# Three runs of score tiles in the projection stage: from behind the first keys to behind the last values of their block

## What is computed

```
q = (layernorm(x) @ Wq + bq)   # 512 queries, 16 heads of 32
k = (y @ Wk + bk)              # 8192 keys
v = (y @ Wv + bv)              # 8192 values
scores = q k^T * scale
attn = softmax(scores, axis=-1)
out = attn @ v ; h = relu(out @ W1 + b1) ; result = h @ W2 + b2
```

## Time and profile before

| | us |
|---|---|
| median of three runs | 1423.57 |
| the profiled execution | 1425.03 |
| its span | 1423.1 |
| PE busy | 1346.2 (95%) |
| DVE busy | 1143.0 (80%) |
| ACT busy | 815.2 (57%) |
| POOL busy | 787.1 (55%) |
| mean granted clock of TensorE | 0.982 |

### The profile page before, as it was taken

One profiled execution on the slowest core, in us unless ns is written; L12 is line 12 of the kernel. 1 busy time (PEld: TensorE's weight loads), 2 busy tenths in 40 slices (PEclk: granted clock), 3 DMA queues, 4 the chain that ended last, 5 costly groups with the idle time before them and its releaser, 6 DMA issues. The chain is left out here.

```text
span 1423.1 us, 39397 instructions
## 1 busy us (share of the span) xinstructions
PE 1346.2 (95%) x16766; PEld 720.1 (51%) x16766; DVE 1143.0 (80%) x1834; ACT 815.2 (57%) x1531; POOL 787.1 (55%) x307
## 2 busy tenths in 40 slices
PE   7989988998999999999999999999999999887898
PEld 4444444443655555555555555555555444556444
DVE  7668877888888888888888888888886664676797
ACT  4445434543777777766776777777777632573212
POOL 3322221222999988998898899989986002000111
PEclk9999999999999999999999999999999999999999
DMA  7567876776352122112212221222120030950000
GB/s 260 169 165 222 231 191 179 214 219 177 93 183 67 38 67 65 52 52 67 63 35 62 65 67 37 68 65 64 40 71 2 18 127 7 202 126 1 1 8 23
DMA packets 127790, 137.44 MB, mean 97 GB/s; under 512 B 44992, under 2 KB 108992, under 8 KB 125696
## 3 DMA queue, kind: packets, MB, share of 16 engines
q1 hardware_dynamic: 127616, 134.93, 33.3%
HBM read 75.66 MB, written 44.17 MB: 84 GB/s over the span
## 5 line engine op out<-in xcount | busy, mean ns | idle before, releaser
L1285 DVE TENSOR_REDUCE early<-attend_banks 128x1 f32<-128x512 f32 x952 | 612.4, 685 | 82.7 <-PE attend_banks L1031 77.5
L1249 ACT ACTIVATE attend_prob<-attend_banks 128x512 f32<-128x512 f32 x1024 | 536.0, 599 | 202.2 <-PE attend_banks L1068 200.0
L1429 POOL TENSOR_TENSOR early<-early,attend_prob 128x1024 f32<-128x1024 f32 x210 | 614.5, 2926 | 37.7 <-ACT attend_prob L1249 9.6
L1068 PE MATMUL attend_banks<-early,k_first 97*32 97x512 f16 x2560 | 261.8, 384 | 3.1 <-ACT attend_prob L1249 3.1
L1031 PE MATMUL attend_banks<-k_first,early 96*32 96x512 f16 x2272 | 236.4, 384 | 1.1 <-PEq L282 1.1
L1031 PE MATMUL attend_banks<-attend_k_rest,early 96*32 96x512 f16 x1536 | 157.6, 380 | 0.0
L1068 PE MATMUL attend_banks<-early,attend_k_rest 97*32 97x512 f16 x1536 | 154.4, 381 | 2.8 <-ACT attend_prob L1249 2.8
L1092 PE MATMUL attend_banks<-attend_prob,ones 128*32 128x128 f32 x3048 | 135.1, 273 | 3.6 <-DVE attend_recip L1297 3.6
L500 POOL TENSOR_TENSOR project_w_whole<-project_grid,project_qscale 128x704 f32<-128x704 f32 x24 | 33.3, 1386 | 183.6 <-DVE project_grid L630 183.6
L1081 PE MATMUL attend_banks<-attend_prob,wkv_area 128*32 128x512 f32 x1024 | 134.8, 592 | 0.0
L1081 PE MATMUL attend_banks<-attend_prob,attend_vh_odd 128*32 128x512 f32 x1024 | 133.7, 592 | 0.0
(11 more groups left out here) (191 smaller groups left out, 1870.4 us busy)
## 6 DMA issues: line engine op xcount, KB each, us to landing
v_scratch<-project_v SPq DMA_DIRECT2D x16, 1024.0 KB, 8.6
early<-in_ctx_dram SPq DMA_DIRECT2D x16, 768.0 KB, 6.1
k_first<-k_scratch SPq DMA_DIRECT2D x36, 256.0 KB, 3.4
k_scratch<-project_k_hi SPq DMA_DIRECT2D x64, 128.0 KB, 3.0
k_scratch<-project_k_lo SPq DMA_DIRECT2D x64, 128.0 KB, 3.1
attend_vh_odd<-v_scratch SPq DMA_DIRECT2D x8, 1024.0 KB, 4.8
wkv_area<-v_scratch SPq DMA_DIRECT2D x7, 1024.0 KB, 4.9
attend_k_rest<-k_scratch SPq DMA_DIRECT2D x24, 256.0 KB, 3.4
```

The lines of the kernel that those rows point to most:

```text
L1068: last = nc.tensor.matmul(s_ps[c * HD:(c + 1) * HD, s_bank[n], :], key_rows[:, c * HD:(c + 1) * HD], q_stack[0:KROWS + 1, h, :], start=Tru ...
L1249: nc.scalar.activation(prob[:, q % PSLOTS, t, :], s_ps[:, s_bank[BT * q + t]], ACT.Exp, scale=SCALE).then_inc(p_ready, 1)
L1285: nc.vector.tensor_reduce(part_max[:, s, j, part:part + 1], pre_ps[:, bank], AX.X, ALU.max).then_inc(pre_read, 1)
L1429: nc.gpsimd.tensor_tensor(sums, sums, prob[:, q % PSLOTS, 0:n], ALU.add).then_inc(pool_summed, 1)
```

## The change

The position KEYS_0 is given up and a position VALUES_3, behind the last value tile, is added. The tiles of head 1's parts 0 and 1 move from KEYS_0 to VALUES_3 of the same blocks, 8 and 10. In block 3 head 0's part 1 goes to VALUES_1 and part 2 to VALUES_3; before they were at KEYS_0 and VALUES_1. VectorE reads the tiles of VALUES_3 in the next block, two behind the low half of key group 0 and its quantization step, two behind group 1's. The tiles of VALUES_3 wait for the low half of the next block's y, as those of VALUES_1 do.

```
-            KEYS_0, KEYS_2, VALUES_1, VALUES_2 = range(4)
-            part_at = {(2, VALUES_1): (0, 0), (3, KEYS_0): (0, 1), (3, VALUES_1): (0, 2), (8, KEYS_0): (1, 0), (10, KEYS_0): (1, 1)}
+            KEYS_2, VALUES_1, VALUES_2, VALUES_3 = range(4)
+            part_at = {(2, VALUES_1): (0, 0), (3, VALUES_1): (0, 1), (3, VALUES_3): (0, 2), (8, VALUES_3): (1, 0),
+                       (10, VALUES_3): (1, 1)}
...
                             key_low(i, u, g)
                             if g < 3:
                                 quantize(1)
-                            if g >= 1:
-                                maxima(b, KEYS_0, range(2 * g - 2, min(2 * g, TT)))
+                            maxima(b - 1, VALUES_3, range(2 * g, min(2 * g + 2, TT)))
                         maxima(b, KEYS_2)
...
-                        pe.wait_ge(ylo_ready, min(b + (2 if place == VALUES_1 else 1), NB))
+                        pe.wait_ge(ylo_ready, min(b + (1 if place == KEYS_2 else 2), NB))
...
                         last.then_inc(k_ready, 1)
-                        if g in (0, 2):
-                            maxima(2 * i + u, (KEYS_0, None, KEYS_2)[g])
+                        if g == 2:
+                            maxima(2 * i + u, KEYS_2)
...
                         last.then_inc(v_ready, 1)
-                        if t in (1, 2):
-                            maxima(2 * i + u, VALUES_1 if t == 1 else VALUES_2)
+                        if t >= 1:
+                            maxima(2 * i + u, (VALUES_1, VALUES_2, VALUES_3)[t - 1])
```

## The result

| | before | after |
|---|---|---|
| median, first comparison (5 runs each), us | 1423.63 | 1413.22 |
| lowest to highest | 1420.21 to 1425.62 | 1412.94 to 1414.64 |
| span of the profiled execution | 1423.1 | 1411.2 |
| mean granted clock | 0.982 | 0.989 |

The account below looks back on a forecast made before the run. TensorE, busy 95% of the span, was taken as the bound, through its idle and slow time. Gains of 3.3, 4.4 and 4.8 us sum to 12.5: 1425.03 becomes 1412.5, less 1.46 for the median gives 1411.1 us, range 1407.0 to 1415.5.

Parts of the forecast that it names:

- The cause: At the transposes of blocks 3, 8 and 10, VectorE's queued score-tile reads are late and hold TensorE, 12.9 us in sum.
- (a) The moved tiles' wait: Moved tiles on TensorE wait for the same block's VALUES_1 reads: 0.90 us in blocks 8 and 10, 0.14 in block 3.
- (b) Block 4: At block 4's transposes, a new wait of 2.1 us replaces the old 3.45; gain 3.3 us over blocks 3 to 5.
- (c) Blocks 9 and 11: At these blocks' transposes, a new wait of 0.75 us; the two pairs gain 4.4 and 4.8 us.
- The clock term: Granted clock does not fall at the new waits; a fall in block 4, up to 2.7 us, had chance 0.13.
- The wait only moves: Rival: reads in blocks 4, 9, 11 stay late, TensorE waits 3.45 to 4.7 us, clock falls; 1423 us, chance 0.07.
- Slower: Rival: in blocks 4 to 11 moved reads delay key stores, so head 0 tiles wait; 1429 us, chance 0.05.
- No new wait: Rival: VectorE's reads come in time, each place costs only its 0.865 us; gain 17.1, time 1406.5 us, chance 0.09.

Follow-up runs that it names:

- block 3 alone: Against the kernel before, only block 3's run of tiles was moved, blocks 8 and 10 keeping theirs behind the first keys; 1421.88 us, ratio 0.9982.
- the runs in blocks 3, 7 and 9: Against the changed kernel, the runs of blocks 8 and 10 put behind the last values of blocks 7 and 9; 1414.32 us, ratio 0.9927 to the kernel before.
- early reads in odd blocks: Against the kernel before, tiles behind the first keys read a key group earlier, runs of blocks 8 and 10 moved to 9 and 11; 1405.8 us, ratio 0.9871.

## Why the prediction was right

**The cause** was right, and is now shown from both sides: early reads at the old place gave 12.7 us, the new place with late reads gave none. The lag of 0.80 us from the start of the third read to the transposes held: 0.79 in block 4 (117.83 to 118.62) and in block 9 (211.16 to 211.95) of the change, 0.79 in block 4 of the new place without early reads.

**(a) The moved tiles' wait** was forecast as 0.90 of delay; it is 0.76 of idle time, which with the 0.16 by which a matmul's record runs over is 0.92. In block 3 the forecast was 0.14; the block takes 18.84 us where 18.64 is its time without a wait (early reads at the old place), so 0.20.

**(b) Block 4.** The replay held step by step. With T = 107.71 (89.91 + 17.80), VectorE after:

```profile
115.84 0.96 DVE L602 TENSOR_TENSOR project_k_lo<-early,project_k_hi 128x512 f16<-128x512 f32 x1
116.72 0.51 DVE L622 TENSOR_SCALAR project_qr<-project_qn 128x704 uint32<-128x704 uint32 x1
117.26 0.53 DVE L624 TENSOR_SCALAR project_qr<-project_qr 128x704 f32<-128x704 f32 x1
117.83 0.69 DVE L646 TENSOR_REDUCE early<-project_yT_ps 128x1 f32<-128x512 f32 x1
```

The low half starts at T + 8.1, the rounder at T + 9.0, the third read at T + 10.1, the transposes (118.62) at T + 10.9, each as forecast. The low half lasts 0.96 instead of 0.68: it starts while GpSimd multiplies (114.86 to 116.24) and ends 0.56 us behind it, as the 1.60 of the earlier trace rows ended 0.55 behind GpSimd's end. The "SBUF — State Buffer" page of the Trainium skill, section "SBUF: two separate sides", says that a GpSimd operation and a VectorE operation with two SBUF inputs exclude each other for a whole instruction; these two rows agree. Gain 3.2 us against 3.3 forecast.

**(c) Blocks 9 and 11.** A delay of 0.75 was forecast; the transposes start at 211.95 where 203.48 + 7.77 = 211.25 would be without a wait, 0.70 (0.53 of idle time in the row, for which the prediction named 0.6 to 0.8). Gains 4.4 and 4.8, as forecast.

**The clock term** was right in part by luck. The forecast took no fall at a wait of 2.1 us, by the nearest row, and gave 0.13 to a fall. Six waits of 1.92 or 1.93 us stand in the profiles of this study (one each in the change's two profiles and with block 3 alone, three with the runs in blocks 3, 7 and 9): the clock fell behind two of them. Of the two waits of 2.09 and 2.10, it fell behind one. So the falls came more often than 0.13 says. The price is 1.7 us, where the prediction bounded it by 2.7. The changed kernel is at the edge here, and an execution of it may well be 1.7 us longer than its profiled one. Of its five runs in the first comparison three had spans of 1411.2 to 1411.4 us at a mean clock of 0.988 or 0.989 and two had 1412.6 and 1412.7 at 0.986; whether block 4 makes this difference was not traced.

**The rivals.** "The wait only moves" is what the place without the reads does: 11.5 us of waits in blocks 4, 9 and 11. It failed because the change also moved the reads up. "Slower" by late stores: the waits that a landing of `k_scratch` ends are two, both in block 15, before as after, 0.58 and 1.19 before, 0.36 and 1.36 after. The stores gained no weight. "No new wait" did not hold for the change, but is what early reads in odd blocks reach: blocks 3 to 5 take 55.19 us there and both pairs 37.39, 17.1 us less than before in sum, as that case has it.

**The size.** 12.5 forecast, and 12.5 and 12.4 in the projection of the two profiles. The whole program gained less: 11.9 between the spans; 9.8 by the ratio and 10.4 by the medians in the first comparison, 11.3 and 11.8 in the second. The interval of the first comparison (up to 12.2) leaves 12.5 out. In its profile the rest of the program was longer by 0.6 us: 0.33 before block 2's keys, which the change does not touch, and 0.3 behind the projection. Over all profiles these keys start between 69.70 and 73.07 us, so nothing ties these tenths to the change. The sum also starts from one execution of the kernel before, of 1425.03 us, and takes it that every execution has the same waits at the same price. The runs on record speak against that: of 17 of them on the second chip the two shortest (1419.94 and 1420.13) are the two with the highest mean clock, 0.986. Whether cheaper falls in such executions account for the missing 1 to 2 us stays open.

## What to carry to other kernels

When PE waits for a bank, look at where the reader's instruction stands in its own queue before moving the producer: reading the tiles one key group earlier gave as much here (12.7 us) as moving tiles and reads (11.3 us). Then put such a filler run where its reader comes in time: with early reads at the old place the third read starts 10.10 us after the keys in block 8, which waited, and 7.73 us after them in block 9, which did not. Replayed from rows of a plain iteration, the three new delays of the change were forecast to 0.1 us. And short waits cost their length: the fastest kernel kept a clock of 1.00 through waits of 0.87 us, and one of 1.64 in block 15, while of the waits of 1.92 us and more at the transposes some cost a slow restart of 1.7 us or more on top.

## What the runs showed of the hardware that was not expected

The granted clock is not decided by the length of a wait alone, in these traces. Waits of 1.92 and 1.93 us were followed by 1.00 (four times) and by 0.64 and 0.71 over the next 3.4 us (twice). With late reads, a wait of 3.45 us in block 9 was followed by 1.00, where the 3.45 us of block 3 in the earlier trace rows was followed by transposes of 2.80 us:

```profile
216.20:219.60 3.40, 0.02 (x1) 0.00 (x0) 3.30 (x8) 1.26 (x2) 1.02 (x2) 1.00 0.40 140
219.60:223.00 3.40, 3.33 (x22) 2.29 (x23) 1.75 (x3) 1.45 (x1) 0.89 (x1) 1.00 0.06 17
```

Nor has a fall one price. Four times the clock was 1.00 through the wait and fell only when PE worked again: block 10 with early reads at the old place, block 11 of the new place without them, blocks 4 and 10 with the runs moved to odd blocks. Each of these cost 1.7 us. In the four waits of 4.7 us the clock fell within the wait, earlier or later. In blocks 8 and 10 of the kernel before and of the one with block 3 alone, the mean clock of the 4.7 us ahead of the transposes was 0.75, 0.84, 0.89 and 0.91, and the pairs took 43.48, 43.92, 44.11 and 44.24 us; by the sum of the prediction the falls cost 2.2, 2.7, 2.9 and 3.0 us. The later in the wait the clock fell, the more of the work behind it was slow. The prediction had only one of these four as its bound. What decides when the clock falls was not tested.

The page "TensorE: Matmul & The Clock Gate" of the Trainium skill, section "Why this matters for your kernels", advises against long idle gaps between bursts; the falls behind 1.93 and 2.10 us and the clock kept behind 3.45 us show that here a gap's length does not say on its own which side it falls on.
